# The expert stage as eight loops with constant weight addresses, and the rounding of the weights shared out anew

## The reference

```python
logits = jnp.einsum('bsh,he->bse', x, w_router)      # x normalised, 2048 tokens, 8 experts
probs = jax.nn.softmax(logits, axis=-1)
sel = jnp.argmax(probs, axis=-1)                      # one expert per token
for e in range(n_experts):
    h = jax.nn.relu(xt @ w1[e] + b1[e])               # 256 -> 1024
    y = h @ w2[e] + b2[e]                             # 1024 -> 256
    m = (sel_t == e).astype(xt.dtype) * wgt_t
    out = out + m[:, None] * y
return x + out
```

## Time and profile before

| | us |
|---|---|
| median of 3 runs | 699.74 (698.88 to 702.32) |
| the profiled execution, by the same clock | 700.6 |
| its span, first to last instruction | 698.8 |
| from the barrier before `experts` to the last matmul | 507.0 to 691.2 |
| PE busy over the span | 593.2 (85%) |
| DVE, POOL, ACT busy | 490.5, 320.8, 292.7 |

### The profile page before, as it was taken

One profiled execution on the slowest core, in us unless ns is written; L12 is line 12 of the kernel. 1 busy time (PEld: TensorE's weight loads), 2 busy tenths in 40 slices (PEclk: granted clock), 3 DMA queues, 4 the chain that ended last, 5 costly groups with the idle time before them and its releaser, 6 DMA issues. The chain is left out here.

```text
span 698.8 us, 12169 instructions
## 1 busy us (share of the span) xinstructions
PE 593.2 (85%) x3679; PEld 512.4 (73%) x3681; DVE 490.5 (70%) x946; ACT 292.7 (42%) x546; POOL 320.8 (46%) x295
## 2 busy tenths in 40 slices
PE   4489999995899999999999985776479899798984
PEld 4478988993688888888888873466358777677873
DVE  4799999974158898898899855774635666655662
ACT  1144545552368778778778711333011211111210
POOL 3434434740025435435435412142164986998263
PEclk9799999996999999999999998865569999989997
DMA  7123411100424223223221004414042352442100
GB/s 226 30 76 93 116 49 31 31 1 15 118 46 91 46 54 84 46 54 83 47 53 39 1 0 159 188 63 186 16 162 80 112 205 80 186 125 84 41 8 4
DMA packets 24070, 54.69 MB, mean 78 GB/s; under 512 B 4840, under 2 KB 9705, under 8 KB 21976
## 3 DMA queue, kind: packets, MB, share of 16 engines
q1 hardware_dynamic: 20328, 46.69, 22.3%
q0 software_dynamic: 2208, 5.41, 2.8%
q10 hardware_dynamic: 1488, 2.05, 1.0%
HBM read 33.14 MB, written 4.87 MB: 54 GB/s over the span
## 5 line engine op out<-in xcount | busy, mean ns | idle before, releaser
L939 POOL TENSOR_SCALAR h_p<-h_p,h_rs 128x1024 f32<-128x1024 f32 x64 | 72.1, 1127 | 116.3 <-DVE h_rs L1042 116.3
L1049 DVE TENSOR_REDUCE h_nmx<-h_psS 128x1 f32<-128x1024 f32 x64 | 78.1, 1221 | 28.8 <-PE h_psS L1141 27.5
L1029 DVE TENSOR_TENSOR h_pTl<-h_psT,h_pTh 128x512 fp32r<-128x512 f32 x128 | 81.5, 678 | 4.4 <-ACT h_pTh L969 4.4
L969 ACT CAST h_pTh<-h_psT 128x512 fp32r<-128x512 f32 x128 | 69.2, 590 | 31.3 <-PE h_psT L1099 31.1
L996 ACT ACTIVATE h_p<-h_psS,h_nmx 128x1024 f32<-128x1024 f32 x64 | 72.2, 1129 | 14.1 <-DVE h_nmx L1049 14.1
L1110 PE MATMUL h_psO<-h_pTh,h_vs 128*128 128x256 f32 x256 | 70.0, 306 | 3.1 <-DVE h_oT L1037 2.3
L1099 PE MATMUL h_psT<-ident,h_p 128*128 128x128 f32 x512 | 67.5, 273 | 1.3 <-DVE h_pTl L1029 1.2
L341 POOL TENSOR_TENSOR a_p<-a_p,a_rs 128x616 f32<-128x616 f32 x32 | 39.0, 1219 | 62.9 <-DVE a_rs L445 62.7
L1099 PEld LDWEIGHTS h_psT<-ident,h_p 128*128 128x128 f32 x512 | 59.2, 141 | 11.2 <-issue 3.3
L1110 PE MATMUL h_psO<-h_pTl,h_vs 128*128 128x256 f32 x256 | 63.6, 282 | 0.0
L1586 POOL TENSOR_TENSOR wl<-wst,wh 128x1024 fp32r<-128x1024 f32 (+1 forms) x18 | 56.0, 3109 | 2.7 <-POOL wh L1583 0.3
(11 more groups left out here) (295 smaller groups left out, 1510.8 us busy)
## 6 DMA issues: line engine op xcount, KB each, us to landing
wst<-in_m_w SPq DMA_DIRECT2D x16, 1024.0 KB
bias<-in_m_b SPq DMA_DIRECT2D x8, 640.0 KB
h_kh<-h_hi SPq DMA_DIRECT2D x30, 128.0 KB, 2.4
h_kl<-h_lo SPq DMA_DIRECT2D x30, 128.0 KB, 2.4
fw<-in_f_w SPq DMA_DIRECT2D x8, 384.0 KB, 3.9
rows<-x_all SPq DMA_DIRECT2D x4, 516.0 KB, 3.4
a_qs<-a_qhi SPq DMA_DIRECT2D x16, 128.0 KB, 2.3
a_qs<-a_qlo SPq DMA_DIRECT2D x16, 128.0 KB, 2.4
```

What stands on the lines that cost most here:

```text
L939: pool.tensor_scalar(pr[:, u % 4], pr[:, u % 4], rs[:, u:u + 1], 0.0, ALU.mult, ALU.add).then_inc(pn_ready, 1)
L969: act.copy(pTh[u // QP % 2][:, hf * HK:(hf + 1) * HK, u % QP * P:(u % QP + 1) * P], psT[hf][:]).then_inc(pT_hi, 1)
L1029: vec.tensor_tensor(pTl[u // QP % 2][part], psT[hf][:], pTh[u // QP % 2][part], ALU.subtract).then_inc(pT_lo, 1)
L1049: vec.tensor_reduce(nmx[:, u:u + 1], psS[u % 2][:], AX.X, ALU.max, negate=True).then_inc(max_ready, 1)
```

## The change

Every engine reads the ends of the eight experts from `table` once, at the start of `experts`, and then runs eight loops, one per expert, with `change(e)` ahead of each. In a loop the expert is a constant, so `load` in the body is gone, the addresses in `hidden` are constants, and `output` takes its address from a register that is moved, not loaded. The first tile of expert 0 stays apart, so expert 0 now has at least two tiles (`steps[:, 0, 1:2]`; it has three here).

ACT rounds all weights: in `change(e)` the second half of e and then the first half of e + 1. DVE subtracts the second half of e in `change(e)`; POOL subtracts only the first half of e + 1 (`split`). PE waits in `change(e)` for both halves of w1's low part at once, and in each tile for w2's low part ahead of `transpose_h`. SP fetches w1 with the bias (`fetch_first`) and w2 (`fetch_second`) apart, each as soon as its part of the buffer is free, and `bias_free` guards the bias. In `context_mlp` POOL has two of its four subtractions left ahead of the gathers.

```diff
-MT = B * S // P + NE - 1
+MT = B * S // P + NE
...
@@ context_mlp, SP
-            fetch_expert(sp, t, io, 0)
-            sp.wait_ge(t["w_in"], 48)
-            fetch_expert(sp, t, io, 1)
+            for e in range(2):
+                fetch_first(sp, t, io, e)
+                fetch_second(sp, t, io, e)
...
-            next_expert(sp, t, io, 2)
+            sp.wait_ge(t["low1"], 2)
+            fetch_first(sp, t, io, 2)
@@ context_mlp, POOL
             power(0)
-            low(0)
+            low_first(pool, t, 0, 0)
             power(1)
-            low(1)
+            low_first(pool, t, 0, 1)
             power(2)
             power(3)
-            low(2)
-            low(3)
...
@@ experts
-            body(0)
-            with eng.Fori(1, load(eng, TILES, MT, NE)) as g:
-                body(g)
+            ends = [load(eng, ENDS + e, MT - (NE - 1 - e), e + 2) for e in range(NE)]
+            change(0)
+            body(0, 0)
+            with eng.Fori(1, ends[0]) as g:
+                body(g, 0)
+            for e in range(1, NE):
+                change(e)
+                with eng.Fori(ends[e - 1], ends[e]) as g:
+                    body(g, e)
@@ SP
-            for e in range(3, NE):
-                next_expert(sp, t, io, e)
+            for e in range(2, NE):
+                if e > 2:
+                    sp.wait_ge(low1, 2 * (e - 1))
+                    if e >= NB:
+                        sp.wait_ge(bias_free, e - NB + 1)
+                    fetch_first(sp, t, io, e)
+                sp.wait_ge(low2, 2 * (e - 1))
+                fetch_second(sp, t, io, e)
@@ POOL, split
-                for part in range(3):
...
-                    pool.tensor_scalar(high, raw, 1.0, 0.0, ALU.mult, ALU.add).then_inc(w_high[part], 1)
...
+                for hf in range(2):
+                    pool.wait_ge(ready, 1)
+                    pool.wait_ge(high1, pool.to_reg(e * 2 + (hf + 3)))
+                    raw, high, low = (halves(w, 1 - par)[:, :, hf] for w in (wst, wh, wl))
+                    pool.tensor_tensor(low, raw, high, ALU.subtract).then_inc(low1, 1)
@@ ACT
+            def change(e):
+                if e == 0:
+                    x_high(0)
+                    return
+                for x in range(2):
+                    high_second(act, t, e, x)
+                if e + 1 < NE:
+                    for hf in range(2):
+                        high_first(act, t, e + 1, hf)
@@ DVE
+            def change(e):
...
+                if e >= 2:
+                    vec.sem_inc(bias_free, 1)
+                for x in range(2):
+                    low_second(vec, t, e, x)
+                vec.wait_ge(in1[e % 2], 32 * (e // 2 + 1))
@@ PE
+            def change(e):
+                if e == 0:
+                    transpose_x(0)
+                pe.wait_ge(low1, 2 * (e + 1))
+            def body(g, e):
                 hidden(g, e)
                 transpose_x(g + 1)
                 if not isinstance(g, int):
-                    output(g - 1, before)
+                    output(g - 1, nc.s_assert_within(pe.snap(second_at), 0, WE))
+                pe.reg_mov(second_at, e % 2 * WE)
+                pe.wait_ge(low2, 2 * (e + 1))
                 transpose_h(g)
@@ helpers
+def high_first(act, t, e, hf):
+    act.wait_ge(t["in1"][e % 2], 32 * (e // 2 + 1))
+    act.copy(halves(t["wh"], e % 2)[:, :, hf], halves(t["wst"], e % 2)[:, :, hf]).then_inc(t["high1"], 1)
+def low_second(vec, t, e, x):
+    vec.wait_ge(t["high2"], 2 * e + x + 1)
+    vec.tensor_tensor(second(t["wl"], e, x), second(t["wst"], e, x), second(t["wh"], e, x),
+                      ALU.subtract).then_inc(t["low2"], 1)
```

More of the change, by code:

```diff
@@ L1525, in experts @@
         ident, table, xg, wst, wh, wl = (t[n] for n in ("ident", "table", "xg", "wst", "wh", "wl"))
-        bias = t["bias"]
+        bias, dst, share, ready = (t[n] for n in ("bias", "dst", "share", "ready"))
         xn = sb("e_xn", [P, D])
@@ L1593, in _ @@
             arrived(pool, t, 2)
-            for i in range(NC + 2, 2 * NC):
-                split_low(pool, t, t["w_high"], i)
+            for hf in range(2):
+                low_first(pool, t, 1, hf)
             for g in range(5, NG):
@@ L1625, in x_high @@
                 act.copy(xh[:], psX[:]).then_inc(xh_ready, 1)
-            x_high(0)
-            def body(g):
+            def change(e):
[5 more added lines that the diff above has]
+                if e + 1 < NE:
+                    for hf in range(2):
+                        high_first(act, t, e + 1, hf)
+            def body(g, e):
                 x_high(g + 1)
@@ L1634, in body @@
                     act.activation(hh[:, hf * FB // 2:(hf + 1) * FB // 2], psT[hf][:], ACT.Relu).then_inc(hh_ready, 1)
-            tiles(act, body)
+            tiles(act, change, body)
         @block.vector
         def _(vec):
-            link = Link(vec, dve)
             def normalise(g):
@@ L1661, in finish, with body @@
                                          ALU.add).then_inc(y_done, 1)
-            normalise(0)
-            x_low(0)
-            normalise(1)
-            def body(g):
-                e = load(vec, g, NE - 1)
+            def change(e):
+                if e == 0:
+                    normalise(0)
+                    x_low(0)
+                    normalise(1)
+                    vec.wait_ge(in1[0], 32)
+                    return
+                if e >= 2:
+                    vec.sem_inc(bias_free, 1)
+                for x in range(2):
+                    low_second(vec, t, e, x)
+                vec.wait_ge(in1[e % 2], 32 * (e // 2 + 1))
+            def body(g, e):
                 for hf in range(2):
@@ L1682, in body @@
                 normalise(g + 2)
-            tiles(vec, body)
-            finish(load(vec, LAST, MT - 1, NE - 1))
+            tiles(vec, change, body)
+            finish(load(vec, LAST, MT - 1, NE))
         @block.tensor
         def _(pe):
+            second_at = pe.alloc_register("e_second_at")
             def transpose_x(g):
@@ L1714, in transpose_h, with output, body @@
                     ins.then_inc(hT_ps, 1)
[L1716 to L1717 removed]
+            def output(g, at):
                 upto(pe, hl_ready, g, 2, 2)
[L1719 removed]
                 for k in range(FB):
[L1721 removed]
                     for n, (h_, w_) in enumerate(((hh, wh), (hl, wh), (hh, wl))):
[L1723 removed]
+                        ins = pe.matmul(psY[:, 0:D], h_[:, k],
+                                        w_[:].rearrange("p a w -> p (a w)")[:, bass.ds(at + (KD * FF + k * D), D)],
                                         start=(k == 0 and n == 0), stop=(k == FB - 1 and n == 2))
                 ins.then_inc(y_ps, 1)
[L1727 to L1731 removed]
+            def change(e):
+                if e == 0:
+                    transpose_x(0)
+                pe.wait_ge(low1, 2 * (e + 1))
+            def body(g, e):
                 hidden(g, e)
@@ L1734, in body, with halves, second, low_first @@
                 if not isinstance(g, int):
-                    output(g - 1, before)
+                    output(g - 1, nc.s_assert_within(pe.snap(second_at), 0, WE))
+                pe.reg_mov(second_at, e % 2 * WE)
+                pe.wait_ge(low2, 2 * (e + 1))
                 transpose_h(g)
-            tiles(pe, body)
-            output(load(pe, LAST, MT - 1, NE - 1), NE - 1)
-def quarter(q):
-    return slice(q * WE // NC, (q + 1) * WE // NC)
-def split_low(eng, t, w_high, i):
-    x, q = divmod(i, NC)
-    part = quarter(q)
-    eng.wait_ge(w_high, i + 1)
-    eng.tensor_tensor(t["wl"][:, x, part], t["wst"][:, x, part], t["wh"][:, x, part],
-                       ALU.subtract).then_inc(t[("w_split", "w1_ready", "w_split", "w_ready")[q]], 2 if q == 1 else 1)
+            tiles(pe, change, body)
+            output(load(pe, LAST, MT - 1, NE), (NE - 1) % 2 * WE)
+def halves(w, par):
+    return w[:, par, 0:KD * FF].rearrange("p (k h f) -> p k h f", k=KD, h=2)
+def second(w, e, x):
+    half = FB * D // 2
+    return w[:, e % 2, KD * FF + x * half:KD * FF + (x + 1) * half]
+def high_first(act, t, e, hf):
+    act.wait_ge(t["in1"][e % 2], 32 * (e // 2 + 1))
+    act.copy(halves(t["wh"], e % 2)[:, :, hf], halves(t["wst"], e % 2)[:, :, hf]).then_inc(t["high1"], 1)
+def low_first(pool, t, e, hf):
+    pool.wait_ge(t["high1"], 2 * e + hf + 1)
+    pool.tensor_tensor(halves(t["wl"], e % 2)[:, :, hf], halves(t["wst"], e % 2)[:, :, hf],
+                       halves(t["wh"], e % 2)[:, :, hf], ALU.subtract).then_inc(t["low1"], 1)
+def high_second(act, t, e, x):
+    act.wait_ge(t["in2"][e % 2], 16 * (e // 2 + 1))
+    act.copy(second(t["wh"], e, x), second(t["wst"], e, x)).then_inc(t["high2"], 1)
+def low_second(vec, t, e, x):
+    vec.wait_ge(t["high2"], 2 * e + x + 1)
+    vec.tensor_tensor(second(t["wl"], e, x), second(t["wst"], e, x), second(t["wh"], e, x),
+                      ALU.subtract).then_inc(t["low2"], 1)
 def gather(pool, t, g):
```

105 lines of the change are left out of this document (36 added, 69 removed).

## The result

| | us |
|---|---|
| median of 4 runs of the changed kernel | 684.12 (682.95 to 684.97) |
| median of 4 runs of the kernel before, same chip | 699.45 (698.88 to 702.32) |
| ratio, 95% interval | 0.9771 (0.9745 to 0.9797) |
| the profiled execution, its span | 682.95, 681.0 |
| PE, DVE, ACT, POOL busy over the span | 583.7, 494.2, 315.0, 271.3 |

The account below looks back on a forecast made before the run. PE was taken to bound the stage, with gaps from its sequencer's loads. The terms -2.1 + 4.4 - 4.2 - 12.6 + 1.1 + 0.7 = -12.7 us took the profiled 700.6 to 687.9, median 687.0, range 679 to 697.

Parts of the forecast that it names:

- Last chunk: End of `context_mlp`: POOL's two late subtractions no longer hold DVE's normalisation, -2.4 us; larger tables +0.3; sum -2.1 us.
- Entry: Start of `experts`: eight loads ahead of everything on PE, DVE and ACT, with nothing to cover them, +4.4 us.
- Tiles 0 and 1: The 2.40 us gap for three loads after tile 0 goes and the clock stays up behind it, -4.2 us.
- Tiles 2 to 19: 18 tiles of 6.83 us plus waits, clock, tile 10 and 1.5 us unexplained: 135.1 us against 147.7, -12.6 us.
- tile 20 to its last output: Third wait, clock, tile, DVE chain and output: 16.7 us against 15.6, +1.1 us.
- The three waits: After one-tile experts 1, 4 and 6, PE waits 3.0 us each in `change` for both of POOL's halves.
- The clock: PE's clock falls to 0.50 behind each wait after a one-tile expert, costing 2.0 us each.
- Tail: At the very end POOL walks through one tile number more, two loads or 0 to 1.4 us: +0.7 us.
- C: Rival: jumps back in the nine loop bodies each wait for a code load, 22 us, 709; chance 0.07.
- D: Rival: PE's sequencer isn't ahead despite missing loads; gaps remain in 18 tiles, 8 us more, 695; chance 0.05.
- A: Rival: the chain at one-tile experts is 0.7 us shorter and the clock stays up, 679; chance 0.16.
- B: Rival: POOL's subtraction gets between DVE's two, delaying the next tile 1.9 us at three changes, 693; chance 0.16.

Follow-up runs that it names:

- r5: Changed kernel with POOL's two late subtractions for expert 0's second half moved back from DVE to POOL in `context_mlp`: 683.49 us, ratio 0.9772 to the kernel before.
- r2: Changed kernel with each loop end loaded just ahead of the change before it is needed, not all eight at the entry: 678.88 us, ratio 0.9701.
- r1: Changed kernel with two unused loads from the table put back at the top of PE's loop body: 693.74 us, ratio 0.9902.
- r7: Changed kernel with POOL's subtraction put ahead of its wait for a gather and its next gather: 682.54 us, ratio 0.9751.
- r9: Changed kernel with late loop ends, PE's wait split by halves and POOL's subtraction ahead of its gather, together: 675.05 us, ratio 0.9700.
- r4: Changed kernel with `hidden` taking its weights' address from a register moved at each change of expert: 685.12 us, ratio 0.9791.
- r3: Changed kernel with PE waiting for w1's low parts half by half inside `hidden`, not for both at the change: 679.41 us, ratio 0.9701.
- r6: Changed kernel with POOL's subtraction of each half of w1 in two instructions of 512 columns instead of one of 1024: 682.09 us, ratio 0.9746.
- r8: Changed kernel with late loop ends, split wait, POOL's subtraction in four pieces and ahead of its gather, together: 676.07 us, ratio 0.9694.

## Why the prediction was right, point by point

1. Last chunk: right, 2.8 us at the tables (503.17 to 500.37) for 2.1. That the held normalisation is the cause is shown by r5 (2.6 us).
2. Entry: right, to 0.1. From the tables to tile 0 6.57 us before, 11.10 after: +4.5 for +4.4. r2 shows that it is the loads, and that it need not be paid.
3. Tiles 0 and 1: -5.3 for -4.2 (from 509.74 to 527.82 before, 511.47 to 524.24 after). The gap and the clock behind it went as said; the two periods are 6.06 and 6.7 us. The 1.1 us more are tile 0: 4.0 us of it lie at the lower clock, before it was 6.0. That was not forecast and is luck of where the clock rose.
4. Tiles 2 to 19, and 5, tile 20 to its last output: I take them together, since the third wait is seen ahead of tile 20's start and not in it. 163.35 us before, 147.86 after: -15.5 for -11.5. The mechanisms were right but for POOL's gather, which was left out; five terms were mis-sized.
   - A quiet tile takes 6.71 us, not 6.83: 18 of them, -2.2. The eight transposes and the step to the next matmul take 0.79, not 0.87, and the sum of 6.79 had been rounded up.
   - The 1.5 us left for what isn't explained weren't there: -1.5. With the loads all "issue" went.
   - The three waits make the tiles before them 3.86, 2.66 and 2.65 us longer, 9.2 for 9.0: +0.2, the sum of two errors. (The idle times listed, 3.63, 2.43 and 2.40, leave out the step to the first matmul.) At tile 11 POOL's pair ran from 4.3 to 9.0 us after the tile's start, where the prediction had 9.6 for its end (its own terms, 4.5 and twice 2.38, give 9.3); at tile 3, with the gather held, from 5.4 to 10.1. The prediction did not have the gather in the chain at all.
   - The clock cost 1.6, 1.35 and 1.5 us at the three waits (against r5's tiles), for 2.0 each: -1.5. In rows 5 to 7 it fell behind idle times of 2.40 and 2.80 and not behind 1.70, so that it would fall was the better reading. But in the changed kernel's second trace it did not fall behind 2.59, in r2 not behind 3.68, and in r5 behind none. That it fell three times in the trace of after is in part luck.
   - Against these, tile 10 took 8.48 us, 1.8 more than a quiet tile, for 0.7: +1.1. The wait is 1.20, inside the prediction's 0.35 to 1.3, but x's transposes and the step behind them, else covered, are added to it.
   - The rest, 0.0 to the last matmul. The last output's idle time is 1.70, as forecast; it also ran at the full clock.
6. Tail: +1.3 for +0.7, the end of POOL's walk.

The sum is -2.8 + 4.5 - 5.3 - 15.5 + 1.3 = -17.8, which is the difference of the spans. The prediction's terms give -12.7, so in the traces they are short by 5.1 us. The medians moved by 15.3, 2.6 more than forecast: the profiled run of before lies 1.2 us over its median of four and that of after 1.2 under its own. That the forecast looks closer by the medians is scatter and no merit of the sum.

Of the rivals, C fell: tiles behind a jump back and tiles behind a change are both 6.71 us apart, and no wait in the stage is for code. The profile's "instruction" queues carried 25 and 26 transfers over the whole span, 21 and 25 before. D fell, and r1 is D made real: 13.5 us in the stage where the prediction put 8, because loads exposed behind the waits and the clock come on top of the gaps. A is half there: two of three waits were 0.6 shorter, but the clock fell. B appeared only in r7 and r9, where POOL had been made to ask sooner.

No run has the eight loops with the old sharing of the rounding, so what the new sharing gave by itself is not shown. PE's waits for low parts did not get shorter with it (8.5 us for 7.6).

## What to carry to other kernels

A load of a value into a register in a loop costs more than its gap: here two of them cost 9.6 to 13.5 us with 6.8 us of gaps; constants in separate loops take them away, but their bounds should be loaded where work is queued, not at the entry. What an engine's sequencer has to do behind a wait is paid in full (r1, r4); loads and register steps belong ahead of the wait, though moving them was not tried. When two engines split weights between them, keep their two-input subtractions away from what was held here (DVE's addition and normalisation, POOL's gather and scatter), and count what the held engine does next. Price a wait by taking its cause away before you reorder around it: POOL's 128x1024 pieces were worth 13 us, and three single edits around them (r3, r6, r7) got 4.4, 1.3 and 0.9.

## What was not expected of the hardware

- An indirect gather keeps POOL for 1.0 us, and for 1.95 or 3.09 beside DVE's pair of subtractions; by its end it then runs behind the first of them or behind both. This is what makes the first wait 2.59 us in one run and 3.63 in another.
- The granted clock fell behind a wait of 2.40 us in one execution and stayed up behind waits of 2.40 to 2.43 us in another (r5), and behind one of 3.68 (r2), with much the same work around them.
- A matmul with its address from a register starts 0.4 us later behind a wait than one with a constant address (2.82 to 2.86 against some 2.41 us), because its register steps stand behind the wait, though in a row of matmuls it costs nothing.
- Two pieces of 128x1024 on POOL take 4.67 to 4.83 us, four of 128x512 take 4.95 to 5.30, and 5.2 and 5.7 where DVE's pair is in the way.
- A DVE operation that one piece of POOL holds isn't always let in at that piece's end: with four pieces one addition was held for 3.73 us (r6) and two for 3.3 (r8), others for 1.5.
